# Moving layer-norm scaling, rms scaling, score-maximum scaling and part of the rotary embedding between VectorE, ScalarE and GpSimd in a one-core decoder block

## The reference

```python
def _layernorm(x, axis=-1, eps=1e-05):
    m = jnp.mean(x, axis=axis, keepdims=True)
    v = jnp.var(x, axis=axis, keepdims=True)
    return (x - m) / jnp.sqrt(v + eps)
...
h = _rmsnorm(x, norm_w)                            # Mamba: rms norm, then projections
xi, z = jnp.split(jnp.einsum('bld,ed->ble', h, in_proj_w), 2, axis=-1)
xi = jax.nn.silu(_causal_depthwise_conv(xi.swapaxes(1, 2), conv_w, conv_b).swapaxes(1, 2))
dt, Bm, Cm = jnp.split(jnp.einsum('bld,ed->ble', xi, x_proj_w), [DT_RANK, DT_RANK + D_STATE], axis=-1)
delta = jax.nn.softplus(jnp.einsum('blr,dr->bld', dt, dt_proj_w) + dt_proj_b)
y = _selective_scan(xi, delta, -jnp.exp(A_log), Bm, Cm, D)   # s = s * exp(delta * A) + delta * B * u
out = jnp.einsum('bld,ed->ble', y * jax.nn.silu(z), out_proj_w) + x
...
def rope(t, cos, sin):                             # cross attention: 8 heads of 32, 128 keys
    return t * cos[None, None] + rotate_half(t) * sin[None, None]
q_a, q_t = rope(q_a, cos_m, sin_m), rope(q_t, cos_m, sin_m)
w = jax.nn.softmax(scores, axis=-1)                # scores = q k / sqrt(32)
x = lin(out, W_o, b_o) + x
x = jax.nn.relu(lin(layernorm(x) * gamma + beta, W_ffn, b_ffn))
...
h = jax.nn.silu(xt @ W1 + B1) * (xt @ W3 + B3)     # 8 experts, the two best of each token, and a shared one
...
x = _layernorm(x + _L0_attn_ref(x, ...))           # x1 in the kernel
x = _layernorm(x + _L0_xattn_ref(x, ...))          # x2; the layer norm inside is xl
x = _layernorm(x + _L0_ffn_ref(x, ...))            # xo
```

## Time and profile before

| | us |
|---|---|
| median of three runs | 1225.23 (1220.23 to 1236.71) |
| span of the profiled execution, first to last instruction | 1224.7 |
| TensorE busy / VectorE / ScalarE / GpSimd | 929.7 / 922.6 / 489.6 / 528.2 |

### The profile page before, as it was taken

The page is one execution under the profiler, slowest core; times in us unless marked ns, Lnnn a source line. Parts: engine busy times, 40 slices in busy tenths (PEclk is TensorE's granted clock), DMA queues, the critical chain, the costliest instruction groups (busy, mean ns, idle before and its releaser), DMA issues.

```text
span 1224.7 us, 13783 instructions
## 1 busy us (share of the span) xinstructions
PE 929.7 (76%) x3960; PEld 700.9 (57%) x3960; DVE 922.6 (75%) x1323; ACT 489.6 (40%) x911; POOL 528.2 (43%) x311
## 2 busy tenths in 40 slices
PE   4845549668689899577689899486789896677996
PEld 2434435256468685165477785165468683554885
DVE  2699996589999966689999965789789965322233
ACT  3534423544246434454345424454245421211442
POOL 1266540453457740533367730544257741001553
PEclk9855558778669999678679899678579997665999
DMA  5100101201023211101023211201023212000331
GB/s 193 36 35 35 52 1 35 70 35 61 18 70 121 77 45 54 70 35 61 18 78 127 73 36 55 85 18 61 18 72 119 86 35 91 21 1 9 117 109 42
DMA packets 38254, 72.61 MB, mean 59 GB/s; under 512 B 3871, under 2 KB 12712, under 8 KB 38174
## 3 DMA queue, kind: packets, MB, share of 16 engines
q1 hardware_dynamic: 38174, 71.65, 17.8%
HBM read 65.14 MB, written 2.30 MB: 55 GB/s over the span
## 4 chain that ended last, share of the span: by engine, by line
PE 45%; DVE 23%; issue 20%; POOL 6%; ACT 3%; DVEq 1%; POOLq 0%; DMA 0%; ACTq 0%; SPq 0%
PE ps L862 11%; DVE hs L1051 7%; PE ps L939 7%; PE ps L718 6%; PE ps L797 5%; POOL dbu L531 4%; DVE yacc L1103 4%; PE ps L836 3%; PE ps L791 2%; PE ps L825 2%; DVE work L1219 2%; PE ps L881 2%; PE ps L776 2%; DVE xn L1014 1%; POOL work L563 1%
## 5 line engine op out<-in xcount | busy, mean ns | idle before, releaser
L531 POOL TENSOR_TENSOR dbu<-v,bbc 128x1024 f32<-128x1024 f32 x128 | 308.9, 2418 | 257.3 <-DVE hs L1051 136.3
L1051 DVE TENSOR_TENSOR_SCAN hs<-ps,carry,dbu 128x512 f32<-128x512 f32 x256 | 313.3, 1266 | 10.1 <-ACT ps L627 8.2
L627 ACT ACTIVATE ps<-delta,neg_a 128x512 f32<-128x512 f32 x256 | 175.7, 692 | 300.5 <-DVE hs L1051 300.4
L718 PE MATMUL ps<-ident,hs 128*128 128x128 f32 x1024 | 189.1, 344 | 116.5 <-DVE yacc L1103 99.5
L718 PEld LDWEIGHTS ps<-ident,hs 128*128 128x128 f32 x1024 | 157.0, 180 | 150.0 <-DVE hs L1051 72.4
L1103 DVE SCALAR_TENSOR_TENSOR yacc<-ps,ctok,yacc 128x512 f32<-128x512 f32 x240 | 167.3, 737 | 1.2 <-PE ps L718 1.0
L555 POOL TENSOR_TENSOR w_lo<-w13s,w_hi 128x512 fp32r<-128x512 f32 x72 | 94.5, 1313 | 145.1 <-ACT w_hi L693 145.1
L939 PE MATMUL ps<-w2s,work 128*128 128x256 f32 x576 | 140.4, 388 | 0.3
L939 PEld LDWEIGHTS ps<-w2s,work 128*128 128x128 f32 x576 | 109.0, 196 | 15.9 <-DVE work L1225 1.5
L1219 DVE SCALAR_TENSOR_TENSOR work<-work 128x512 f32<-128x512 f32 x72 | 82.3, 1143 | 46.5 <-POOL work L563 45.6
L862 PE MATMUL ps<-x_hi,w_hi 128*128 128x512 f32 x288 | 107.9, 457 | 9.4 <-DVE work L1225 9.2
(11 more groups left out here) (159 smaller groups left out, 1243.0 us busy)
## 6 DMA issues: line engine op xcount, KB each, us to landing
w13s<-in_w SPq DMA_DIRECT2D x72, 256.0 KB, 2.9
bbc<-brow_dram SPq DMA_DIRECT2D x32, 512.0 KB, 4.0
w2s<-in_w SPq DMA_DIRECT2D x36, 256.0 KB, 2.7
cbc<-comb_dram SPq DMA_DIRECT2D x32, 256.0 KB, 3.5
work<-work SPq DMA_DIRECT2D x16, 256.0 KB, 2.3
xn<-in_x SPq DMA_DIRECT2D x5, 512.0 KB, 5.3
xt<-in_x SPq DMA_DIRECT2D x4, 512.0 KB, 3.6
rope<-in_rope_q SPq DMA_DIRECT2D x4, 512.0 KB, 4.2
```

The source lines that it names most:

```text
L531: pool.tensor_tensor(dbu[:, i % DRING, :, :], v[:, 2 * h:2 * h + 2, :], bbc[:, n // 2 % 2, n % 2, :].rearrange("p (o t) -> p o t", o=1) .t ...
L627: act.activation(ps[:, unit % 2, :], delta[:, q, :], ACT.Exp, scale=neg_a[:, q * NS + m:q * NS + m + 1]).then_inc(da_done.sem, 1)
L718: last = pe.transpose(ps[:, bank, t * P:(t + 1) * P], src(t), ident[:, :])
L1051: dve.tensor_tensor_scan(hs[:, m % 2, q, 0:TC], ps[:, unit % 2, :], dbu[:, n % DRING, q % 2, :], carry[:, m, q:q + 1], ALU.mult, ALU.add). ...
```

## The change

The rms scaling goes to ScalarE (a `Copy` with a scale per row), as does the last step of the layer norms (an `Identity` with a scale and a bias per row; the bias, minus the mean times the reciprocal deviation, is a new product of 128x4 on GpSimd, and VectorE prepares minus the mean), and the scaling of the score maxima. In the rotary embedding VectorE takes the cosine product straight from PSUM with the bias in the same instruction, four of 128x512 in the late part of `T_Q`; GpSimd does the sine product and the sum. In the diff `act`, `pool` and `dve` at the head of a call name the engine. The new calls of `normalise` in `T_LNT` and `T_X2T` stand in the mid part of the tick, where VectorE had them, the one in `T_OUT` in the late part; the scaling of the maxima stands in the early part of `T_PT + 2 * tile`.

```diff
+        qc = [work[:, 4096:5120].rearrange("p (b t) -> p b t", b=2), x1t]
...
-        cos_done = signal("cos_done", 2)
+        cos_done = signal("cos_done", HB)
...
+                pool.wait_ge(*norm[k]["rstd"].at(j, 1))
+                pool.tensor_tensor(shift[k][:, :], less[k][:, :], rstd[k][:, :], ALU.mult
+                                   ).then_inc(norm[k]["shift"].sem, 1)
...
                             pool.tensor_tensor(qs[:, b, :], qs[:, b, :], rope_part(1), ALU.mult
                                                ).then_inc(sin_done.sem, 1)
+                            pool.wait_ge(*sin_done.at(j, s + 1))
+                            pool.wait_ge(*cos_done.at(j, 2 * s + 2))
+                            pool.tensor_tensor(qr[:, b, :], qc[s][:, :, :], qs[:, b, :], ALU.add).then_inc(q_done.sem, 1)
...
+                if kind == "fetch" and n == 3:
+                    act.wait_ge(*rms_done.at(j, 1))
+                    for t in range(NT):
+                        last = act.activation(xn[:, t, :], xn[:, t, :], ACT.Copy, scale=rms[:, t:t + 1])
+                    last.then_inc(xn_done.sem, 1)
...
+                if kind == "post" and n == 5:
+                    normalise(j, "x1", x1, x1_done)
...
+            def normalise(j, k, tiles, after):
+
+                act.wait_ge(*norm[k]["shift"].at(j, 1))
+                for t in range(NT):
+                    act.activation(tiles[:, t, :], tiles[:, t, :], ACT.Identity, scale=rstd[k][:, t:t + 1],
+                                   bias=shift[k][:, t:t + 1]).then_inc(after.sem, 1)
...
+                    if t == T_LNT:
+                        normalise(j, "xl", xa, xl_done)
+                    if t == T_X2T:
+                        normalise(j, "x2", x2, x2_done)
...
+                    if t == T_OUT:
+                        normalise(j, "xo", xa, fin_done)
...
                     if t == T_PT + 2 * tile:
+                        act.wait_ge(*mx_done.at(j, tile + 1))
+                        act.activation(top[:, :], mx[:, :], ACT.Copy, scale=-HD ** -0.5).then_inc(top_score_done.sem, 1)
                         act.wait_ge(*top_score_done.at(j, tile + 1))
...
-                if kind == "fetch" and n == 3:
-                    if is_first(j):
-                        dve.wait_ge(consts.sem, 5 + CHUNKS)
-                    dve.wait_ge(*rms_done.at(j, 1))
-                    for t in range(NT):
-                        last = dve.tensor_scalar(xn[:, t, :], xn[:, t, :], rms[:, t:t + 1], None, ALU.mult)
-                    last.then_inc(xn_done.sem, 1)
...
-                if kind == "post" and n == 5:
-                    normalise(j, "x1", x1, x1, x1_done)
...
+                dve.tensor_scalar(less[k][:, :], mean[:, :, 0], -1.0, None, ALU.mult).then_inc(norm[k]["less"].sem, 1)
...
-            def normalise(j, k, src, dst, after):
-                mean = mv[k][:, :].rearrange("p (t n) -> p t n", t=NT)
-                dve.wait_ge(*norm[k]["rstd"].at(j, 1))
-                for t in range(NT):
-                    dve.tensor_scalar(dst[:, t, :], src[:, t, :], mean[:, t, 0:1], rstd[k][:, t:t + 1],
-                                      ALU.subtract, ALU.mult).then_inc(after.sem, 1)
...
-                if t == T_ROT:
-                    for s in range(2):
-                        b = slice(2 * s, 2 * s + 2)
-                        if s == 0:
-                            dve.wait_ge(*rope_in.at(j, 16))
-                        dve.wait_ge(*qs_in[s].at(j, 32))
-                        dve.tensor_tensor(qr[:, b, :], qr[:, b, :], rope_part(0), ALU.mult).then_inc(cos_done.sem, 1)
-                    for s in range(2):
-                        b = slice(2 * s, 2 * s + 2)
-                        dve.wait_ge(*cos_done.at(j, s + 1))
-                        dve.wait_ge(*sin_done.at(j, s + 1))
-                        dve.tensor_tensor(qr[:, b, :], qr[:, b, :], qs[:, b, :], ALU.add).then_inc(q_done.sem, 1)
+                if t == T_Q:
+                    dve.wait_ge(*rope_in.at(j, 16))
+                    for b in range(HB):
+                        dve.wait_ge(*(q_ps.at(j, HB) if b >= 2 else q_ps.at(j, b + 1)))
+                        dve.wait_ge(*q_rows.at(j, b + 1))
+                        dve.scalar_tensor_tensor(out=qc[b // 2][:, b % 2, :], in0=ps[:, 4 + b, :], scalar=col("bq", b),
+                                                 in1=rope[:, 0, :], op0=ALU.add, op1=ALU.mult).then_inc(cos_done.sem, 1)
...
+                        dve.wait_ge(*top_score_done.at(j, tile))
                         dve.tensor_reduce(mx[:, :], s8, AX.X, ALU.max).then_inc(mx_done.sem, 1)
-                        dve.wait_ge(*mx_done.at(j, tile + 1))
-                        dve.wait_ge(*p_done.at(j, tile))
-                        dve.tensor_scalar(top[:, :], mx[:, :], -HD ** -0.5, None, ALU.mult
-                                          ).then_inc(top_score_done.sem, 1)
```

More of the change, by code:

```diff
@@ L215, in block_kernel @@
         carrier = sb("carrier", [1, 8])
-        stat, mv, ve, rstd = ({k: sb(f"{name}_{k}", [P, NT * n]) for k in ("x1", "xl", "x2", "xo")}
-                              for name, n in (("stat", 6), ("mv", 2), ("ve", 1), ("rstd", 1)))
+        stat, mv, ve, less, rstd, shift = ({k: sb(f"{name}_{k}", [P, NT * n]) for k in ("x1", "xl", "x2", "xo")}
+                                           for name, n in (("stat", 6), ("mv", 2), ("ve", 1), ("less", 1), ("rstd", 1),
+                                                           ("shift", 1)))
         row_v = yacc[0:1, 0, :]
@@ L287, in block_kernel @@
         x1_done = signal("x1_done", NT)
-        norm = {k: {s: signal(f"{k}_{s}", n) for s, n in (("stats", NT), ("held", 1), ("aggr", NT), ("ve", 1), ("rstd", 1))}
+        norm = {k: {s: signal(f"{k}_{s}", n) for s, n in (("stats", NT), ("held", 1), ("aggr", NT), ("less", 1), ("ve", 1), ("rstd", 1),
+                                                      ("shift", 1))}
                 for k in ("x1", "xl", "x2", "xo")}
@@ L1158, in second_mid @@
                     deviations(j, "xl")
-                if t == T_LNT:
-                    normalise(j, "xl", xa, xa, xl_done)
                 if t == T_X2:
                     relu_rows(j, 0)
-                if t == T_X2T:
-                    normalise(j, "x2", x2, x2, x2_done)
                 if t == T_TOP:
@@ L1234, in second_late @@
                     deviations(j, "xo")
-                    normalise(j, "xo", xa, xa, fin_done)
             def wide(a):
```

## The result

The changed kernel takes 1157.16 us (median of four runs, 1151.82 to 1160.23) against 1225.44 (1220.23 to 1236.71) in the same comparison: ratio 0.9394, 95% interval 0.9351 to 0.9437, 68 us faster where 45 were forecast. The profiled span fell from 1224.7 to 1157.2.

What follows compares the result with a forecast made beforehand. The prediction took VectorE operations held up beside GpSimd as the loss. Three bodies of 15.4 us gave 46.2, body 0 and start 5.5, less 2.0 and 4.6: net 45.1, from 1224.7 to 1179.6, forecast 1180, range 1166 to 1204.

Steps and rivals of the forecast that it cites:

- the inner norm's term: At `xl`, before the feed-forward: VectorE gets 5.0 us back, but TensorE limits the gain to 3.3 a body (2.0 to 5.0).
- The clock: Rival on TensorE's two clock levels: two more slow chunks make 1191 (0.20 with colliding sums), all fast 1165 (0.13).
- The rival nearest to the result: All clocks fast, with full gains at the maxima and rms scaling: 1165 us, chance 0.13.
- x2: Layer norm ahead of the experts: ScalarE ends its scaling 1.0 earlier, scans move up 3.3; gain 2.3 us a body.
- Rms scaling: Experts: 4.0 us gained per middle body (3.4 to 6.0); body 0 4.5, the start 1.
- The maxima: Attention stage: VectorE loses four scalings, 2.6 us and the waits around them; 2.0 a body counted (1.0 to 3.4).
- Rotary embedding: Between queries and scores: four GpSimd operations of 2.32 us let scores start 3.8 earlier a body (0 to 4.5).
- the dear sums: Rival in the rotary stage: a GpSimd sum takes twice VectorE's 2.55 us, giving 1202; chance 0.04.
- the colliding ones: Rotary stage: GpSimd's operations collide and take 3.4 us each, no gain there, 1196; chance 0.20 shared with two slow clocks.
- The loop's turn: Two turns: ScalarE's copies stand behind `xo`'s scaling, so the input projection starts 1.0 us later each (0 to 3).
- The last chunk: Behind the loop, GpSimd hardly runs: four norms cost 4.0 us in all, the rotary stage about 0.6.
- ScalarE: Rival: ScalarE's added work ahead of the decays holds the recurrence's scans, a loss of 11.6 us, 1237; chance 0.04.

Runs made afterwards that it cites:

- p_ts: Changed kernel with four useless VectorE scaling instructions of 128x256 added at the inner norm's tick: 1183.46 us, ratio 0.9619.
- u_xl: Changed kernel with the last step of the inner layer norm `xl` alone back on VectorE: 1174.07 us, ratio 0.9528.
- only_xl: Kernel before with only the last step of the inner norm `xl` moved to ScalarE: 1203.62 us against 1232.89, ratio 0.9761.
- u_x2: Changed kernel with the last step of the layer norm `x2` alone back on VectorE: 1164.90 us, ratio 0.9454.
- u_rms: Changed kernel with the rms scaling alone back on VectorE: 1188.72 us, ratio 0.9632.

## Why the forecast was too high

Stretch lengths in means of three profiles of the kernel before (1224.7, 1241.4, 1232.8) and two of the changed one (1157.2, 1167.3), from their timelines:

| stretch | before | after | gain | forecast |
|---|---|---|---|---|
| start and body 0, to chunk 1's first copy | 192.7 | 185.3 | 7.4 | 5.5 |
| input projection to queries, x3 | 24.9 | 24.4 | 1.8, with 0.4 ahead of it | 0 |
| queries to scores (rotary), x3 | 25.8 | 22.0 | 11.2 | 11.4 |
| attention (maxima), x3 | 58.3 | 55.3 | 8.9 | 6.0 |
| last residual to feed-forward (`xl`), x3 | 14.8 | 9.8 | 14.9 | 9.9 |
| feed-forward to last relu, x3 | 11.6 | 7.5 | 12.2 | 0 |
| relu to experts (`x2`), x3 | 15.0 | 10.9 | 12.2 | 6.9 |
| experts (rms scaling), x3 | 117.4 | 113.7 | 10.8 | 12.0 |
| loop's turn, x2 | 10.0 | 10.3 | -0.6 | -2.0 |
| last chunk, behind the loop | 209.6 | 217.9 | -8.3 | -4.6 |
| whole span | 1233.0 | 1162.3 | 70.7 (rows: 70.5) | 45.1 |

**The step that failed is the inner norm's term**: "Next late is TensorE with the feed-forward, so I count TensorE's 3.3". The mechanism named there was right (VectorE held beside GpSimd, ScalarE not), and the transposes of `xl` did start 3.4 us earlier, 6.6 behind the last residual instead of 10.0 in every turn. But next late was VectorE again: between these transposes and the feed-forward stand the scan's, which had waited 1.04 us for the VectorE that was now free (`p_ts` shows this way by itself). So the feed-forward started 5.0 earlier a body (`u_xl`, `only_xl`). And with `xl` moved the feed-forward ran at full clock, another 4.1 a body in the mean (`only_xl`), where the sum had nothing. With 1.0 lost in the last chunk that is 26 us for a term of 8.9, 17 of the 26 us by which these means miss the forecast. On the first two profiles alone (1224.7 and 1157.2), the one before with a single turn at half clock, the wait gives 15.1 and the feed-forward 7.0: 21 for 8.9, 12 of 22. The clock stood among the rivals as something that shifted waits turn either way; for this stage it went one way. The rival nearest to the result, 1165 with all clocks fast, still held `xl` and `x2` at their capped terms.

**`x2`** was mis-sized too (4.1 instead of 2.3), but the experts' first tick and the last chunk took more than half back; `u_x2` measured 8 by the runs, where the forecast's term was 5.9. **Rms scaling** was right in kind, a little low in body 0 and at the start (7.2 by `u_rms` for 5.5); in the experts its 4.6 (`u_rms`) less the 1.9 given back behind `x2` would be 2.7 a body, where the table has 3.6. **The maxima** gave 3.0 in the means for 2.0; against the kernel before at like clock it is 1.0 (57.5 and 56.5 at 0.80) to 2.7 (56.3 and 53.6 at 0.85), so part of the 3.0 is clock.

**Rotary embedding**: right to 0.1 us; the sums took 2.34, so neither the dear sums nor the colliding ones happened. The rule of the Trainium skill (GPSIMD Engine Reference, Engine selection), that elementwise adds belong on VectorE with GpSimd about twice as slow, agrees with the trace where GpSimd stands idle: VectorE's sum then took 1.21 us, GpSimd's 2.34. Its advice does not hold here, since beside GpSimd VectorE's took 3.36. The 2.55 that the forecast read as the price beside GpSimd is the mean of five of 3.36 and three of 1.21, and the dear rival's doubling of it, 5.1, stands in no row.

**The loop's turn** cost 0.3 in the mean, and 0.1 where both ran at full clock (9.5 to 10.2 against 9.6 to 9.9), not 1.0: ScalarE was back in 0.75 after the jump, not 2.22, and its copies ended 0.66 us before the input projection began (445.65 + 1.26 against 447.57), right behind TensorE's own output projection. **The last chunk** lost 8.3 instead of 4.6: 1.0 to 1.1 at each norm (the forecast's 4.0), 0.6 in the rotary stage, 2.0 in the experts, whose start came at a lower clock (0.95 for 0.98), and 1.5 in attention, whose length in the last chunk wandered (46.5 to 53.2 in the kernel before, 49.0 and 53.2 in the changed one). **ScalarE** never held the recurrence (1.0 us of waits in 256 scans).

What stays open: what decides the clock of single executions in attention, what in the move of `xl` keeps the feed-forward from half clock, and how the smaller parts add. Undoing parts one by one cost 16.9, 7.7, 31.6, 19.7 and 18.6 by the runs, 94 together with `x1` and `xo` still moved, for a gain of 68; part of that is the clock, and the rest was not taken apart.

## What to carry to other kernels

Moving a VectorE instruction that is held beside GpSimd frees the whole time that it was held, for what waits for its result and for what stands behind it in VectorE's list. Follow both ways to the next stage, through the order of the other engines' lists: here the second was worth 1.6 of the 5.0 us a body. Cap the gain by another engine only where a row shows that engine waiting for nothing. Ask also which stage starts behind the shortened wait and whether it ran at half clock: that stage can gain nearly as much again, and a single profile may show its lucky case. Freed time in front of a stage that starts at half clock comes back only in part.
